# Decoder with local attention: scores and weighing each moved into one run of TensorE's program

## What is computed

```python
        def attn_layer(x, Wqkv, qs, ksc, Wo):
...
            q = l2norm(q) * qs
            k = l2norm(k) * ksc
...
            q = q * cos * scale + rotate_half(q) * sin * scale
            inv = 1.0 / scale
            k = k * cos * inv + rotate_half(k) * sin * inv
            out = local_attention(q, k, v)
            out = out.transpose(0, 2, 1, 3).reshape(b, n, INNER)
            return out @ Wo

        for i in range(DEPTH):
            x = attn_layer(shift_tokens(x), Wqkv[i], q_scale[i], k_scale[i], Wo[i]) + x
            x = ffn_layer(shift_tokens(x), ln_g[i], ln_b[i], W1[i], b1[i], W2[i], b2[i]) + x
```

## Time and profile before

| | |
|---|---|
| median of 3 runs | 2076.47 us (2074.24 to 2077.68) |
| the profiled execution | 2077.16 us, span 2075.4 us |
| PE (matmuls) busy | 1973.1 us, 95% |
| VectorE / ScalarE / GpSimd busy | 68% / 67% / 52% |
| granted TensorE clock, mean | 0.989 of full speed |
| chain that ended last | PE 88%, ScalarE 5%, VectorE 4%, issue 3% |
| scores, PE busy | 169.1 us in 12288 passes |
| weighing, PE busy | 167.6 us in 12288 passes |

### The profile page before, as it was taken

One profiled execution on the slowest core, in us unless ns is written; L12 is line 12 of the kernel. 1 busy time (PEld: TensorE's weight loads), 2 busy tenths in 40 slices (PEclk: granted clock), 3 DMA queues, 4 the chain that ended last, 5 costly groups with the idle time before them and its releaser, 6 DMA issues.

```text
span 2075.4 us, 74512 instructions
## 1 busy us (share of the span) xinstructions
PE 1973.1 (95%) x32424; PEld 1171.9 (56%) x32424; DVE 1407.7 (68%) x1975; ACT 1393.9 (67%) x2125; POOL 1086.2 (52%) x709
## 2 busy tenths in 40 slices
PE   8989897789999999999999999999999999999997
PEld 5655654355555555555555655555555555555553
DVE  1454545677777777777777777777777787777762
ACT  5565564466777667776777677767776777677763
POOL 1000000496666666666666666666666666666650
PEclk9999998799999999999999999999999999999999
DMA  3000001132223222232222323222332223222220
GB/s 118 2 1 1 2 21 31 28 77 64 63 63 94 73 73 63 64 94 73 73 63 66 92 71 78 74 60 72 85 79 73 67 63 95 73 74 63 64 63 21
DMA packets 82210, 128.37 MB, mean 62 GB/s; under 512 B 17246, under 2 KB 28124, under 8 KB 81884
## 3 DMA queue, kind: packets, MB, share of 16 engines
q1 hardware_dynamic: 81884, 123.59, 22.9%
HBM read 21.81 MB, written 1.05 MB: 11 GB/s over the span
## 4 chain that ended last, share of the span: by engine, by line
PE 88%; ACT 5%; DVE 4%; issue 3%; DMA 0%; ACTq 0%; SPq 0%; DVEq 0%
PE ps L621 17%; PE ps L617 16%; PE ps L643 9%; PE ps L697 9%; PE ps L682 7%; PE ps L689 7%; PE ps L427 4%; PE ps L626 3%; PE ps L662 3%; PE ps L630 3%; DVE work L1254 2%; PE ps L523 2%; PE ps L441 1%; PE ps L655 1%; PE ps L650 1%
## 5 line engine op out<-in xcount | busy, mean ns | idle before, releaser
L1424 POOL TENSOR_TENSOR work<-work,RS 128x1024 f32<-128x1024 f32 x192 | 365.2, 1902 | 386.3 <-ACT RS L969 384.6
L1101 DVE TENSOR_TENSOR work<-ps,work 128x512 f32<-128x512 f32 (+1 forms) x288 | 247.7, 860 | 328.9 <-ACT work L1029 292.3
L621 PEld LDWEIGHTS ps<-ident,work 128*128 128x128 f32 x3072 | 342.8, 141 | 141.3 <-issue 104.7
L621 PE MATMUL ps<-ident,work 128*128 128x128 f32 x3072 | 394.2, 275 | 6.3 <-ACT work L997 2.4
L1443 POOL TENSOR_TENSOR work<-work 128x1024 f32<-128x1024 f32 x96 | 225.9, 2354 | 99.0 <-DVE work L1106 99.0
L1435 POOL TENSOR_TENSOR work<-work 128x1024 f32<-128x1024 f32 x96 | 227.2, 2367 | 69.1 <-DVE work L1106 69.1
L1106 DVE TENSOR_TENSOR work<-ps,work 128x512 f32<-128x512 f32 (+1 forms) x288 | 247.2, 858 | 0.0
L1041 ACT ACTIVATE work<-work 128x1024 f32<-128x1024 f32 x96 | 101.5, 1057 | 205.1 <-DVE work L1186 204.7
L1146 DVE TENSOR_REDUCE SS<-work 128x16 f32<-128x1024 f32 x192 | 232.0, 1208 | 0.0
L689 PEld LDWEIGHTS ps<-work 64*32 64x32 f32 x12288 | 134.8, 105 | 147.7 <-issue 132.9
L617 PE MATMUL ps<-WQ,XS 128*128 128x512 f32 x384 | 189.3, 616 | 8.0 <-issue 4.4
(11 more groups left out here) (184 smaller groups left out, 3091.8 us busy)
## 6 DMA issues: line engine op xcount, KB each, us to landing
work<-work SPq DMA_DIRECT2D x576, 128.0 KB
work<-work SPq DMA_DIRECT2D x336, 64.0 KB
WQ<-in_wqkv SPq DMA_DIRECT2D x6, 512.0 KB, 3.6
WK<-in_wqkv SPq DMA_DIRECT2D x6, 512.0 KB, 4.5
WV<-in_wqkv SPq DMA_DIRECT2D x6, 512.0 KB, 3.5
WO<-in_wo SPq DMA_DIRECT2D x6, 512.0 KB, 3.8
work<-ZR SPq DMA_DIRECT2D x48, 64.0 KB
W<-in_w SPq DMA_DIRECT2D x6, 341.0 KB, 3.2
```

What stands on the lines that cost most here:

```text
L621: m = nc.tensor.transpose(flat(R)[:, t * 128:t * 128 + 128], src[:, t * 128:t * 128 + 128], ident[:, :])
L1101: V.tensor_tensor(h16(cos_part[:, j, cols]), h16(src), rotary_tabs[:, at:at + 64].unsqueeze(1).broadcast_to([PARTS, heads_in, 64]), ALU.mu ...
L1424: U.tensor_tensor(h16(qk_norm[:, j, :]), h16(cos_part[:, j, :]), inv_norms[:, j, :].unsqueeze(2).broadcast_to([PARTS, 16, 64]), ALU.mult). ...
```

## The change

On TensorE alone, calls stand in another order. The scores of a block are made in one go, before the probabilities of the block ahead are turned. The FFN pieces follow, then the queries' projection of the next block, and then the whole weighing. The queries' projection gets a wait for `probs_turned_copied`, since it overwrites the bank from which the turned probabilities are copied; the weighing's waits move with it. The number of calls and what they compute is unchanged, and so is every other engine's program.

```diff
@@ -673,7 +673,6 @@
                 par0 = (n - 1) % 2
                 nb = (n - 1) % 4
 
-
                 def scores(first, last):
                     for c8 in range(first, last):
                         for q in range(2):
@@ -743,12 +742,10 @@
                     pe.wait_ge(mask_seeded, g)
                     if n == 3:
                         pe.wait_ge(keys_carried, (g + 1) // 4)
-                    scores(0, 4)
+                    scores(0, 8).then_inc(scores_ready, 1)
                 if c:
                     pe.wait_ge(probs_ready, g - 1)
                     turn(bank_z, probs[:, :, :, :].rearrange('p c a b -> p (c a b)')).then_inc(probs_turned, 1)
-                if b:
-                    scores(4, 8).then_inc(scores_ready, 1)
                 if f is not None and n == 0:
                     variance(f)
                 if f is not None and n == 1:
@@ -757,12 +754,6 @@
                     project_out(fo, 0, 2)
                 if fo is not None and n == 3:
                     project_out(fo, 6, 7)
-                if c:
-                    if a:
-                        pe.wait_ge(k_sin, 2 * g + 2)
-                    pe.wait_ge(probs_turned_copied, g - 1)
-                    pe.wait_ge(windows_loaded, 160 * (g - 1))
-                    weigh(0, 4)
                 if fo is not None and n == 2:
                     project_out(fo, 2, 3 if fo < FFN_PASSES - 1 else 8)
                 if fo is not None and n == 3:
@@ -770,9 +761,15 @@
                 if g + 1 < ALL_BLOCKS:
                     if not b:
                         pe.wait_ge(q_sin, g + 1)
+                    if c:
+                        pe.wait_ge(probs_turned_copied, g - 1)
                     queries(g + 1)
                 if c:
-                    weigh(4, 8).then_inc(heads_weighed, 1)
+                    if a:
+                        pe.wait_ge(k_sin, 2 * g + 2)
+                    pe.wait_ge(probs_turned_copied, g - 1)
+                    pe.wait_ge(windows_loaded, 160 * (g - 1))
+                    weigh(0, 8).then_inc(heads_weighed, 1)
 
 
             def last_centre(b):
```

## The result

| | before | after |
|---|---|---|
| median (lowest to highest), 20 runs of each on one chip | 2077.22 us (2073.05 to 2082.17) | 2088.26 us (2073.30 to 2099.78) |
| profiled execution, its span | 2077.16, 2075.4 | 2085.81, 2084.0 |
| granted clock, mean | 0.989 | 0.98 |

The ratio is 1.0061, with a 95% interval of 1.0050 to 1.0072: the change makes the kernel slower by 0.6%; the two medians lie 11 us apart. (Ratios leave out one execution of a later experiment, at 3761.47 us, which is far from all its others.) The forecast was 2054, with 2032 to 2072 as its range. The time lies outside it, on the other side of no change.

The account below looks back on a forecast made before the run. TensorE's own sequence, busy 95% of the span, was taken as the bound. Layer blocks -31, early blocks +2 and instruction supply +6 gave -23 us from a median of 2076.47, so 2054, range 2032 to 2072.

Parts of the forecast that it names:

- Whole runs at 1.42: Scores and weighing on TensorE: two halves at 1.58 become one run at 1.42, twice, saving 0.32 us a block.
- Turn 0.97, pieces 1.72, queries 1.81: Whole-array work with fewer tile-run borders: turn saves 0.05 us, FFN pieces 0.20, next queries 0.11 a block.
- The copy's wait, 0.3 in n=0 only: Queries wait 1.13 us for ScalarE's copy of turned probabilities; FFN pieces cover it except some 0.3 in n=0.
- No gain in n=0: Block kind n=0 counted as zero gain: PE's saving ends in the wait for VectorE's gating in n=1.
- 0.32 given back twice a group: Waits for the head copy (n=1 to n=2) and rotated queries (n=3 to n=0) each give back 0.32 us.
- Early blocks +2: Six blocks with a turn but no FFN pieces have the copy's wait bare: +2 us, at most +4.
- Instruction supply, +6, bounds -8 and +25: Late instruction packets at whole tile runs: 17 to 20 stalls of 1.2 us, 20 to 24 against 18.0 now.
- instruction supply takes over: Rival: 256-instruction runs regularly outrun their packets on TensorE, making the kernel slower, 2104 us in its example; chance 0.10.
- The other engines follow: Rival: the give-backs at the head copy and rotated queries don't bind, 66 blocks gain 0.68 us, 2040; chance 0.15.
- Whole runs are slow: Rival: whole scores runs take 1.62 us, losing 13 of the 31 us gained, 2067; chance 0.10.
- the bound is a chain already: Rival: a K projection, rotation and softmax chain through VectorE binds every block; no change, 2073 to 2081; chance 0.07.

Follow-up runs that it names:

- second experiment: On the changed kernel, scores put back into two halves around the probabilities' turn, weighing left whole behind the queries: 2053.65 us, ratio 0.9900 to before.

## Why the prediction was wrong

By its steps:

1. *Whole runs at 1.42.* Right for weighing, 1.41, and for the scores of n=1; the scores of the other kinds take 1.49 to 1.52. The 1.62 of the first block was no pace of whole runs.
2. to 4. *Turn 0.97, pieces 1.72, queries 1.81.* Right: 0.93, 1.72, 1.81. The gross gain of 0.68 a block stands in n=1 to n=3 as 0.72, 0.66 and 0.64. Why a border costs its 0.1 was not tested.
5. *The copy's wait, 0.3 in n=0 only.* Right in size: 0.25 in an undisturbed block,

```profile
1206.01 1.98 PE L617 MATMUL ps<-WQ,XS 128*128 128x512 f32 x4 [0.25 <-ACT work L1031]
```

and 9.3 us in 23 waits in all, of which the early blocks without a piece have the long ones (up to 1.1).

6. *No gain in n=0.* Right by the number, 14.64 and 14.53, and by luck. The reason given was that a gain in n=0 ends in a wait for the gating in n=1. In after PE hardly waits there (L626 for L1093: 2.8 us in 6 waits); its n=0 is no shorter because the scores run takes 1.52 and the copy's wait lies in it. The reason does hold where n=0 gets shorter, in the second experiment: there it is 14.27, and then in n=1

```profile
1262.88 1.13 PE L626 MATMUL ps<-YN,W 128*128 128x512 f32 x2 [0.38 <-DVE work L1095]
```

7. and 8. *0.32 given back twice a group.* The mechanism is there and the price was too high. PE waits for L956 14 times, 2.5 us, and for L1103 9 times, 4.2 us: 6.7 us against the 14 in the sum. In the block shown, the heads' turn starts 2.04 behind the value projection instead of 1.82, so 0.22 late.
9. *Early blocks +2.* They have +10. In the stretch from 396.06 to 460 the granted clock was 0.99 before; of after the row is

```profile
396.06:460.00 63.94, 52.19 (x1053) 31.30 (x1052) 46.35 (x58) 39.88 (x65) 51.97 (x33) 0.93 0.28 68
```

with PE at half clock for 6.8 us from 421.9, and again from 469.7. I had priced a wait there and no clock. The copy's wait can't be parted from the stalls in these blocks.

10. *Instruction supply, +6, bounds -8 and +25.* **This is the step that failed.** The mechanism was the right one and the size was not. Waits for "issue" before scores, weighing and transposes went from 18.0 to 47.6: +30, beyond the upper bound. Three parts of the working were wrong. It took each packet to come some 3.4 us after the last; that is the shortest distance of two packets in the layers of after (3.35), but in block 56 no packet moved for over 8 us ahead of the run, and the one that was wanted began only with the run, 3.1 us before PE went on. It took a bad start to lie within 8 places ahead of a border to 20 behind, one in ten; the table shows 15 ahead to 60 behind, though not for every run there. And it took 1.2 us a stall, where n=0 has 1.4 to 2.6. It also held scores and weighing to be alike; weighing hardly stalls. In the measure of the blocks the sum was -31 + 2 + 6; measured it is -47 for undisturbed groups, +10 for the early blocks and +44 of excess, so that the other steps were too cautious by 16 us and this one with what hangs on it took far more than that.

What lies around the stalls was in no term: the clock that falls after some of them, and VectorE's chain, which begins with the maximum of the complete scores and so stands through each stall. The excess is +44 and the early blocks +10, where the stalls themselves are +30. At half clock the layers of after spend 30.6 us more than those of before (6.8 us twice and 3.4 five times), which can't cost more than half of that, 15 us. How the remaining 24 or so divide between the clock and the engines that follow was not measured.

Of the rivals the true one is *instruction supply takes over*, which had 0.10. Its reasoning held: a 256-record run outruns its packet, and each stall is longer than before. Its evidence was in the rows, the stall of 1.26 inside one of only three whole runs, and deserved more weight: only three of the things to be built stood in the trace, and two of them were not good. The bound for it, 0.15 us a run in 192 runs, was just reached by the stalls alone: 30 us are 0.16. The Trainium skill (Runtime: NRT & Kernel Launch, Instruction fetch mechanics) has the fetch hidden behind issue; the 47.6 us here disagree. The Trainium skill's Advanced Engine Details and Errata (ISA Cache) speaks of only two lines of 256 instructions, but the same place gives TensorE 128 KB, which at 16 KB a line would be eight. The traces side with the two: no transfer begins more than 44 records ahead of the border before its own. *The other engines follow* was nearly right for undisturbed blocks (2.12 a group, where it had three times 0.68) and is not what decided. *Whole runs are slow* and *the bound is a chain already* were not seen.

The second experiment comes out at 2053.65, where I had forecast the whole change. That is no success of the sum, since the steps summed were those of both runs made whole.

**What stays open.** What decides whether a packet is asked for ahead of the scores' wait or behind it: the two are told apart in the traces, but no run here sets the cause apart, nor the share of the data traffic in it. Why the new order with scores whole has more packets behind the wait than scores whole alone. Why the same 1.02 us of the turn removes stalls of over 2 us (block 76: 2.55 in after, 0.36 in the second experiment). And why weighing runs hardly stall.

## What to carry to other kernels

Count a dense stretch in instructions as well as in microseconds: where 256 of them pass in 1.4 us, as here, the engine can outrun its own program, and "issue" in the waits is the sign to price first. In this kernel it paid to leave slow whole-array work inside the stretch, in its first half, and to merge the other run. Here merging the weighing alone gives 1.0% and merging the scores as well takes it back.

And when a change is a bundle, forecast its parts apart, and don't expect them to add up: on the kernel before, weighing alone gains 23 us and scores alone lose 16, which would be a gain of 6; together they lose 11. With weighing already whole, the scores cost 35.

## What was not expected of the hardware

- All "issue" gaps of PE in the layers stand at one remainder of its record count by 256, within two, in both kernels; the program moved by 48 records has as many of them before scores (23 and 22) in other blocks.
- From the start of a packet's transfer to PE's next instruction it took 2.2 to 3.1 us at all 65 such gaps in the layers of before and after (3.1 in block 56 of after, 2.4 at the stall of the earlier trace rows), and the transfer never begins more than 44 records ahead of the border before.
- In the layers of after the packet of a scores run begins either ahead of the end of the scores' semaphore wait or 1.0 to 2.0 us behind it (starts 1 to 59 places behind a border); the first went without a stall 5 times in 5, the second stalled 16 times in 16.
- A stall of over 2 us was followed by 3.4 us at a granted clock of 0.54; 6 of 11 such stalls were. In the kernel before, the layers have no stretch at the lower level but the first 6.8 us, at 390.5; after the change there are seven more.
- Two kernels with the same tile runs, 112 and 16 passes, differ by 24 us, by which of them comes first.
